# Three cross-attentions in eight-head units with 32-row score matmuls, each step's transposes issued first

## The chip, the cores and the metric

The kernel runs on one core of one Trainium2 chip. The metric is the device time of one execution in microseconds (us): the median of the runs shown, smaller is better. A kernel here is one program in which five engines run their own instruction streams at the same time: TensorE (PE, matmuls; PEld is its weight load), VectorE (DVE), ScalarE (ACT), GpSimd (POOL) and SyncE (SP, which only issues transfers). They meet at semaphores.

## What is computed

A decoder of four layers over 16 sequences of 128 tokens, width 128. Each layer is self-attention (or a recurrence), cross-attention and feed-forward, every one of them added to x behind a layer norm. The change touches the cross-attentions of layers 0, 1 and 2 (called L0x, L1x, L2x): 16 heads of 8 features each, keys and values from a context `ctx`.

```python
qh, kh, vh = heads(q @ Wq + bq), heads(ctx @ Wk + bk), heads(ctx @ Wv + bv)   # L0x: relu, no bias
scores = einsum('bhqd,bhkd->bhqk', qh, kh) / sqrt(8)
scores = where(mask, -1e9, scores)                                            # L1x only
out = einsum('bhqk,bhkd->bhqd', softmax(scores), vh)
x = x + out @ Wo + bo                                                         # L0x: x + out
```

## The kernel before

All of x stays in SBUF (`X`). The phases in `PHASES` run one after another; every phase goes over four groups (`GROUPS`) of four sequences, three in a hardware loop and the last written out.

**A unit.** In L0x, L1x and L2x a group is 16 units, one for each sequence i and each block g of four heads. The query weights are laid out so that head 4g+j stands in rows 32j to 32j+7 of its own 128-row block, so queries and keys take four projections each (`keys`, `queries`), and `KD` holds the keys as a block pattern on zeros: 12 copies of 32 rows on ACT (L1034) and 4 on DVE (L1346) for each group write it. For one unit PE does one float32 matmul with 128 contraction rows and 512 columns (`scores1`, L550; in L1x a bf16 matmul adds the mask ahead of it, L549), DVE takes the row maximum (`take_max`, L1268) and subtracts it (`shift`, L1280), ACT does the exponential (L999), PE transposes the four 128x128 blocks (`transpose_p`, L559), ACT copies them out of PSUM (L1008), and PE multiplies each by the head's values (`product_v`, L579; a column of ones in `VE` gives the sum). A float32 matmul shows as two records, a transpose as one.

**The order on each engine** is written by hand. PE, in step u: scores of unit u+3, transposes of u+1, product of u. The scores rotate over three PSUM banks, so PE's next scores never wait for the exponential of the unit before. ACT: exponential of u+1, then the copy of u. DVE: maximum of u+1, then the subtraction of u, and `normalise` for each sequence. At the end of a group come the next group's projections and the copies into `KD`; the next group's first scores wait for them.

**Between phases.** POOL clears `KD` ahead of L0f and ahead of L1x (L490). The mask of L1x is loaded when L1a is done, and the context of L1x is queued on SP behind it. POOL converts the mask for each group (L513). Rows that are masked in full are mended on DVE in L1x (L1276, L1289, L1291) with one more matmul (L582).

## Time and profile before

| what | us |
|---|---|
| median of 2 runs (lowest, highest) | 2348.39 (2346.02, 2350.75) |
| the profiled execution | 2347.53 |
| its span in the trace | 2345.5 |
| PE busy | 1660.7 (71%) |
| DVE busy | 1427.9 (61%) |
| ACT busy | 879.8 (38%) |
| POOL busy | 91.5 (4%) |
| L0x, from the last x of L0a to its own last x | 196.8 |
| L1x, likewise | 236.9 |
| L2x, likewise | 207.0 |

The time of the profiled execution is its span and 2.0 us around it. A busy share is a mean over phases with different limits: the recurrence of layer 3 hardly uses PE, the attentions hardly leave it idle. The granted clock (PEclk) is TensorE's clock as a share of 2.4 GHz; 0.5 is the lower level, 1.2 GHz. In a timeline row the idle time ahead of an instruction stands in brackets with what ended it.

### The profile page before, as it was taken

How to read it: one execution, taken by the hardware profiler on the slowest of the kernel's cores; microseconds unless marked ns; L12 is line 12 of the kernel's file. 1: busy time of each engine (PE TensorE's matmuls, PEld its weight loads, DVE VectorE, ACT ScalarE, POOL GpSimd, SP SyncE). 2: the span in 40 equal slices, each digit the busy share in tenths (PEclk: the TensorE clock that was granted, in tenths of full speed). 3: DMA queues.
4: the chain of work that ended last, by engine and by line, in shares of the span. 5: the costliest groups of instructions: out<-in, count | busy, mean ns of one | idle time of the engine just before them, and what ended most of it. 6: DMA issues, size and time to landing. Idle time of an engine off the chain costs nothing.

```text
span 2345.5 us, 29947 instructions
## 1 busy us (share of the span) xinstructions
PE 1660.7 (71%) x9244; PEld 1220.6 (52%) x9244; DVE 1427.9 (61%) x4030; ACT 879.8 (38%) x1409; POOL 91.5 (4%) x82
## 2 busy tenths in 40 slices
PE   5988989997368888869995369899988880000366
PEld 4876876664237557646663247656666440000244
DVE  4544445667865655647776864556657536999445
ACT  4455354563333443434443432255544331010022
POOL 1000000001000000010000100000000000000001
PEclk9999999998679999989996675999989995555568
DMA  2000003000000000000000000000000012000100
GB/s 97 1 0 0 0 1 128 5 4 1 0 0 1 0 0 0 0 14 5 4 5 1 0 0 0 0 5 9 0 1 0 15 29 73 1 1 1 45 9 18
DMA packets 19262, 27.92 MB, mean 12 GB/s; under 512 B 3184, under 2 KB 14320, under 8 KB 18288
## 3 DMA queue, kind: packets, MB, share of 16 engines
q1 hardware_dynamic: 19184, 27.02, 3.4%
q8 instruction: 31, 0.51, 0.1%
q14 instruction: 47, 0.39, 0.1%
HBM read 21.51 MB, written 5.51 MB: 12 GB/s over the span
## 4 chain that ended last, share of the span: by engine, by line
issue 59%; PE 22%; DVE 13%; DVEq 2%; ACT 1%; POOL 1%; DMA 1%; SPq 0%; POOLq 0%; ACTq 0%
PE PSA L550 3%; PE PSA L579 3%; PE PSA L883 2%; PE PSA L559 2%; PE PSA L802 2%; DVE W L1736 2%; DVE W L1725 2%; DVE BIG L1729 1%; PE PSA L819 1%; DVE BIG L1732 1%; PE PSA L622 1%; PE PSA L856 1%; PE PSA L846 1%; PE PSA L778 1%; DVE W L1710 1%
## 5 line engine op out<-in xcount | busy, mean ns | idle before, releaser
L1268 DVE TENSOR_REDUCE MX<-PSA 128x4 f32<-128x512 f32 x320 | 220.9, 690 | 273.2 <-PE PSA L550 129.6
L579 PEld LDWEIGHTS PSA<-VE,PR 128*128 128x128 f32 x2048 | 252.7, 193 | 25.1 <-issue 17.1
L579 PE MATMUL PSA<-VE,PR 128*128 128x9 f32 x2048 | 258.4, 254 | 0.1
L999 ACT ACTIVATE TMP<-TMP 128x512 f32<-128x512 f32 x160 | 100.8, 630 | 338.6 <-DVE TMP L1280 338.6
L550 PE MATMUL PSA<-BIG,QK 128*128 128x512 f32 x384 | 202.2, 615 | 11.1 <-DVE QK L1352 11.1
L910 PE MATMUL PSA<-W,TMP 128*128 128x128 f32 x32 | 8.3, 441 | 263.5 <-DVE TMP L1761 263.5
L1008 ACT ACTIVATE PR<-PSA 128x512 f32<-128x512 f32 x320 | 186.5, 583 | 7.2 <-PE PSA L559 6.6
L999 ACT ACTIVATE PQ<-PQ 128x512 f32<-128x512 f32 x160 | 100.7, 629 | 179.4 <-DVE PQ L1280 179.4
L910 PEld LDWEIGHTS PSA<-W,TMP 128*128 128x128 f32 x32 | 7.1, 327 | 264.6 <-DVE TMP L1761 264.6
L559 PE MATMUL PSA<-K,TMP 128*128 128x128 f32 x640 | 100.5, 279 | 33.0 <-ACT TMP L999 32.2
L559 PEld LDWEIGHTS PSA<-K,TMP 128*128 128x128 f32 x640 | 71.5, 140 | 100.5 <-ACT TMP L999 97.3
L474 POOL TENSOR_TENSOR RSTD<-VEPS,HALF 128x4 f32<-128x4 f32 x50 | 50.4, 1007 | 1576.4 <-DVE VEPS L1241 1576.4
L1280 DVE TENSOR_TENSOR TMP<-PSA,MX 128x512 f32<-128x512 f32 x160 | 109.3, 683 | 2.5
L1280 DVE TENSOR_TENSOR PQ<-PSA,MX 128x512 f32<-128x512 f32 x160 | 109.3, 683 | 2.4
L1034 ACT ACTIVATE BIG<-PSA,COLS 32x512 f32<-32x512 f32 x144 | 97.6, 678 | 32.3 <-PE PSA L622 28.9
L765 PE MATMUL PSA<-K,BIG 128*128 128x128 f32 x128 | 31.7, 414 | 107.8 <-DVE BIG L1473 107.8
L539 PE MATMUL PSA<-QK,BIG 128*128 128x128 f32 x512 | 103.2, 283 | 3.5 <-DVE BIG L1370 3.5
L994 ACT ACTIVATE XNT<-PSA 128x512 f32<-128x512 f32 x44 | 26.1, 593 | 212.0 <-PE PSA L528 212.0
L559 PEld LDWEIGHTS PSA<-K,PQ 128*128 128x128 f32 x640 | 73.8, 142 | 60.9 <-ACT PQ L999 56.2
L559 PE MATMUL PSA<-K,PQ 128*128 128x128 f32 x640 | 99.2, 278 | 4.2 <-ACT PQ L999 4.2
L541 PE MATMUL PSA<-I,BIG 128*128 128x128 f32 x512 | 99.0, 275 | 0.0
L680 PE MATMUL PSA<-W 128*128 128x256 f32 x256 | 66.5, 425 | 41.6 <-ACT W L401 39.5
(309 smaller groups left out, 3436.4 us busy)
## 6 DMA issues: line engine op xcount, KB each, us to landing
CTX<-in_ctx_t SPq DMA_DIRECT2D x16, 256.0 KB, 3.1
W<-in_w SPq DMA_DIRECT2D x1, 2048.0 KB, 7.3
ROWS<-in_rows SPq DMA_DIRECT2D x1, 1744.0 KB, 12.2
W<-in_w SPq DMA_DIRECT2D x2, 768.0 KB, 9.4
W<-in_w SPq DMA_DIRECT2D x1, 1412.0 KB, 14.3
W<-in_w SPq DMA_DIRECT2D x2, 640.0 KB, 10.0
W<-in_w SPq DMA_DIRECT2D x2, 512.0 KB, 12.5
scratch_q<-BIG SPq DMA_DIRECT2D x4, 256.0 KB, 2.4
```

The lines of the kernel that those rows point to most:

```text
L474: pool.tensor_tensor(RSTD[:, 0, :], VEPS[:, 0, :], HALF[:], ALU.pow).then_inc(ln_rstd.sem, 1)
L539: pe.matmul(bank[:, tok(j)], KD[:, u, j, :], KT[:, g, tok(i)], start=True, stop=False, skip_group_check=True)
L541: mm = pe.matmul(bank[:, tok(j)], POS[:, u, j, :], I2[:], start=False, stop=True, skip_group_check=True)
L550: mm = pe.matmul(bank, QT[:, g, tok(i)], KD[:, u].rearrange("p j t -> p (j t)"), start=p != "L1x", stop=True, skip_group_check=True)
L559: mm = pe.transpose(PS[4 + u % 2][:, tok(j)], PQ[u % 2][:, tok(j)], ident)
L579: mm = pe.matmul(dst, PR[:, u % 2, tok(j)], val, start=True, stop=True)
L680: mm = pe.matmul(PS[1 + c % 4][:, tok(n, 256)], pe_table[:, P - 1 - 4 * m:2 * P - 1 - 4 * m], QB[:, m].rearrange("p r h -> p (r h)"), star ...
L999: act.activation(PQ[u % 2], PQ[u % 2], ACT.Exp, scale=scale).then_inc(exp_ready.sem, 1)
L1008: act.activation(PR[:, u % 2, :], PS[4 + u % 2], ACT.Copy).then_inc(p_ready.sem, 1)
L1034: act.activation(KD.rearrange("p (i g) j t -> p i g j t", g=HG)[r, :, g, j, :], tile(PS[K_BANK[g]][r]), func, bias=col(f"{p}.bk", g)[r]).t ...
L1268: dve.tensor_reduce(MX[:, tok(u % 4, 4)], tile(PS[1 + u % 3]), AX_X, ALU.max).then_inc(max_taken.sem, 1)
L1280: dve.tensor_tensor(tile(PQ[u % 2]), tile(PS[1 + u % 3]), last(m, P), ALU.subtract).then_inc(shifted.sem, 1)
```

## The change

For L0x, L1x and L2x the units are replaced; the other phases keep their code.

- A unit has eight heads of one sequence: 8 units a group (`HALVES`), 32 a phase, all written out with no hardware loop. The weights are no longer padded: one projection each for keys and queries. POOL writes `KM` from the projected keys `KN`, four copies of 128x512 with all but one head in four zeroed (`masked_keys`), so that two float32 matmuls of 32 contraction rows and 512 columns, on neighbouring 32-row strips and into two banks, give the eight heads' scores. Four banks hold two units' scores.
- DVE's maximum and subtraction and ACT's exponential work on 128x1024. Transposes and PSUM copies stay at 512, two to a unit, through banks 4 and 5, one each.
- PE's step m is: transposes of unit m+1, scores of unit m+2, product of unit m. ACT's is: exponential of m+1, copies of m. Everything else (projections, next norm's transposes, outputs) has its place in a step, over bank 7, and groups follow one another without a break. Keys, values and queries have two buffers.
- The mask is loaded at the start and converted once, in L0a. Rows masked in full get queries of zero (`SOME`, computed in L0x), which takes the mending operations and the matmul L582 out of L1x. POOL's clearing ahead of L1x moves ahead of L1f.

The core of the diff:

```diff
+                    sp.dma_start(MASK1[:], mask1.rearrange("b o q k -> q (b o) k")).then_inc(masks_loaded, 16)
             for p in run:
-                if p == "L1x":
-
-                    if run[0] != p:
-                        sp.wait_ge(x_updated.sem, x_updated.before[p])
-                    sp.dma_start(MASK1, mask1.rearrange("b o q k -> q (b o) k")).then_inc(masks_loaded, 16)
...
+            def masked_keys(p, new):
+
+                pool.wait_ge(k_ready.sem, k_ready.at(p, new))
+                for r in range(4):
+                    ins = pool.tensor_scalar(KM[:, new % 2, :, r, :], tile(KN[:, new % 2, :]), col("lane", r), None, ALU.mult)
+                ins.then_inc(km_ready.sem, 1)
...
-                if p in ("L0f", "L1x") and p != run[0]:
+                if p in ("L0f", "L1f") and p != run[0]:
 
                     pool.wait_ge(x_updated.sem, x_updated.before[p])
                     pool.memset(BIG[:, 0:8192], 0.0).then_inc(kd_zero, 1)
...
+                if p == "L0a":
+                    pool.wait_ge(masks_loaded, 32)
+                    pool.tensor_copy(MKB[:], MASK1[:]).then_inc(mask_ready, 1)
+                if p in CROSS3:
+                    ln_root(p, 0)
+                    for new in range(GROUPS):
+                        masked_keys(p, new)
+                        if new:
+                            ln_root(p, new)
+                    continue
...
-                else:
-                    if p == "L1x":
-                        pe.matmul(tile(bank), NEGI[:], mid(MKB[:, i, :]), start=True, stop=False, skip_group_check=True)
-                    mm = pe.matmul(bank, QT[:, g, tok(i)], KD[:, u].rearrange("p j t -> p (j t)"), start=p != "L1x", stop=True,
-                                   skip_group_check=True)
...
+                def scores(m):
+                    it, e = m // HALVES, m % HALVES
+                    i, h = e // 2, e % 2
+                    if e == 0:
+                        pe.wait_ge(q_ready.sem, q_ready.at(p, it))
+                        pe.wait_ge(km_ready.sem, km_ready.at(p, it))
+                    if m >= 2:
+                        pe.wait_ge(shifted.sem, shifted.at(p, 0, m - 2))
+                    banks = [PS[2 * (m % 2) + n] for n in range(2)]
+                    if p == "L1x":
+                        for n in range(2):
+                            pe.matmul(tile(banks[n]), NEGI[:], mid(MKB[:, it * GB + i, :]), start=True, stop=False, skip_group_check=True)
+                    for n in range(2):
+                        r = strip_of(2 * h + n)
+                        mm = pe.matmul(banks[n], QN[r, it % 2, tok(i)], KM[r, it % 2, i].rearrange("p r t -> p (r t)"),
+                                       start=p != "L1x", stop=True, skip_group_check=True)
+                    mm.then_inc(s1_psum.sem, 1)
+
+                def transposes(m):
+                    pe.wait_ge(exp_ready.sem, exp_ready.at(p, 0, m))
+                    for c in range(2):
+                        if m:
+                            pe.wait_ge(p_ready.sem, p_ready.at(p, 0, 2 * (m - 1) + c))
+                        for j in range(4):
+                            mm = pe.transpose(PS[4 + c][:, tok(j)], PH[:, m % 2, tok(4 * c + j)], ident)
+                        mm.then_inc(t_psum.sem, 1)
+
+                def product(m):
+                    it, n, h = m // HALVES, m // 2, m % 2
+                    if m % HALVES == 0:
+                        pe.wait_ge(v_ready.sem, v_ready.at(p, it))
+                    if h == 0 and n:
+                        pe.wait_ge(on_ready.sem, on_ready.at(p, 0, n - 1))
+                    for c in range(2):
+                        pe.wait_ge(p_ready.sem, p_ready.at(p, 0, 2 * m + c))
+                        for j in range(4):
+                            head = 8 * h + 4 * c + j
+                            mm = pe.matmul(PS[6][:, 9 * head:9 * head + 9], PT[:, m % 2, c, tok(j)],
+                                           VE2[:, it % 2, n % GB, head, :], start=True, stop=True)
+                    mm.then_inc(pv_done.sem, 1)
...
+                project_keys(0, PS[4])
+                project_queries(0, PS[5])
+                project_values(0, PS[6])
+                scores(0)
+                scores(1)
+                transposes(0)
+                for m in range(GROUPS * HALVES):
+                    it, e = m // HALVES, m % HALVES
+                    if m + 1 < GROUPS * HALVES:
+                        transposes(m + 1)
+                    if m + 2 < GROUPS * HALVES:
+                        scores(m + 2)
+                    product(m)
+                    more = it + 1 < GROUPS
+                    if e == 0 and more:
+                        project_keys(it + 1, misc())
+                        freed = k_ready, k_ready.at(p, it + 1)
...
+                def exp(m):
+                    act.wait_ge(shifted.sem, shifted.at(p, 0, m))
+                    act.activation(PH[:, m % 2, :], PH[:, m % 2, :], ACT.Exp, scale=float(HD) ** -0.5).then_inc(exp_ready.sem, 1)
+
+                def copies(m):
+                    if m >= 2:
+                        act.wait_ge(pv_done.sem, pv_done.at(p, 0, m - 2))
+                    for c in range(2):
+                        act.wait_ge(t_psum.sem, t_psum.at(p, 0, 2 * m + c))
+                        act.activation(PT[:, m % 2, c, :], PS[4 + c], ACT.Copy).then_inc(p_ready.sem, 1)
...
+                keys(0, PS[4])
+                if p != "L1x":
+                    queries(0, PS[5])
+                exp(0)
+                for m in range(GROUPS * HALVES):
+                    if m + 1 < GROUPS * HALVES:
+                        exp(m + 1)
+                    copies(m)
+                    if m:
+                        after(m - 1)
...
+                def softmax_inputs(m):
+                    s = PSA[:, 2 * (m % 2):2 * (m % 2) + 2, :].rearrange("p n (r t) -> p (n r) t", r=4)
+                    high = MX[:, 8 * (m % 2):8 * (m % 2) + 8]
+                    dve.wait_ge(s1_psum.sem, s1_psum.at(p, 0, m))
+                    dve.tensor_reduce(high, s, AX_X, ALU.max).then_inc(max_taken.sem, 1)
+                    dve.wait_ge(max_taken.sem, max_taken.at(p, 0, m))
+                    if m >= 2:
+                        dve.wait_ge(t_psum.sem, t_psum.at(p, 0, 2 * (m - 2) + 1))
+                    dve.tensor_tensor(tile(PH[:, m % 2, :], 8), s, last(high, P), ALU.subtract).then_inc(shifted.sem, 1)
...
+                values(0, PS[6])
+                next_moments(p, 0)
+                for u in range(GROUPS * HALVES):
+                    it, e = u // HALVES, u % HALVES
+                    softmax_inputs(u)
+                    if u == 0:
+                        next_normed(p, 0)
+                    if e == 0 and it:
+                        values(it, PS[7])
+                    if u >= 3 and u % 2:
+                        normalise(u // 2 - 1)
...
+                    if e == 5 and it and p != "L0x":
+                        update(it - 1)
+                    if e == 5 and p == "L1x" and it + 1 < GROUPS:
+                        queries(it + 1, PS[7])
+                    if e == 5 and it + 1 < GROUPS:
+                        next_moments(p, it + 1)
+                    if e == 7 and it + 1 < GROUPS:
+                        next_normed(p, it + 1)
```

## Rows read from the trace of the kernel before

**Rows 1.** Stage windows, the three cross-attentions; columns as the first line names them

```profile
core 0: us, PE busy (x) PEld busy (x) DVE busy (x) ACT busy (x) POOL busy (x), PEclk, DMA share, GB/s
377.10:573.90 196.80, 183.54 (x1008) 123.02 (x1008) 127.13 (x252) 107.28 (x181) 4.03 (x4) 0.99 0.10 41
1027.30:1264.20 236.90, 210.24 (x1152) 143.34 (x1152) 158.64 (x373) 111.31 (x193) 13.34 (x9) 0.95 0.03 7
1529.55:1736.50 206.95, 191.82 (x1056) 129.97 (x1056) 131.10 (x269) 109.67 (x185) 4.03 (x4) 0.97 0.01 4
```

**Rows 2.** Timeline, group starts in L0x: start us, us, engine, line, operation

```profile
389.35 0.69 DVE L1268 TENSOR_REDUCE MX<-PSA 128x4 f32<-128x512 f32 x1 [1.29 <-PE PSA L550]
390.20 0.69 DVE L1268 TENSOR_REDUCE MX<-PSA 128x4 f32<-128x512 f32 x1 [0.17 <-PE PSA L550]
...
437.66 0.69 DVE L1268 TENSOR_REDUCE MX<-PSA 128x4 f32<-128x512 f32 x1 [1.29 <-PE PSA L550]
```

**Rows 3.** Timeline, one steady step of L0x on the four engines

```profile
411.29 1.10 PE L550 MATMUL PSA<-BIG,QK 128*128 128x512 f32 x2
...
412.23 0.60 PE L559 MATMUL PSA<-K,PQ 128*128 128x128 f32 x4
412.43 0.69 DVE L1268 TENSOR_REDUCE MX<-PSA 128x4 f32<-128x512 f32 x1 [1.04 <-PE PSA L550]
...
412.67 1.05 PE L579 MATMUL PSA<-VE,PR 128*128 128x9 f32 x8
413.04 0.68 DVE L1280 TENSOR_TENSOR TMP<-PSA,MX 128x512 f32<-128x512 f32 x1
...
413.58 1.10 PE L550 MATMUL PSA<-BIG,QK 128*128 128x512 f32 x2
...
413.76 0.63 ACT L999 ACTIVATE TMP<-TMP 128x512 f32<-128x512 f32 x1 [1.21 <-DVE TMP L1280]
...
414.29 0.58 ACT L1008 ACTIVATE PR<-PSA 128x512 f32<-128x512 f32 x1
414.44 0.45 PEld L559 LDWEIGHTS PSA<-K,TMP 128*128 128x128 f32 x4 [0.58 <-ACT TMP L999]
```

**Rows 4.** Groups by form, wide operations elsewhere; count | busy, mean ns | idle before

```profile
L1571 DVE TENSOR_TENSOR QK<-PSA,K 128x1024 f32<-128x1024 f32 x8 | 9.8, 1221 | 3.9 <-PE PSA L778 3.9
...
L1116 ACT COPY BIG<-QK 32x1024 f32<-32x1024 f32 x16 | 16.7, 1042 | 3.1 <-DVE QK L1575 2.8
```

**Rows 5.** Timeline of DVE, the end of L1x: two dependent operations

```profile
1258.07 0.25 DVE L1295 RECIPROCAL RD<-OS 128x16 f32<-128x16 f32 x1
1258.40 0.29 DVE L1297 TENSOR_TENSOR ON<-OS,RD 128x128 f32<-128x128 f32 x1
```

**Rows 6.** Timeline, the start of L1x and POOL's first job in L1f

```profile
1027.37 6.92 POOL L490 MEMSET BIG<- 128x8192 f32 x1 [3.61 <-DVE X L1263]
...
1032.56 5.75 PE L622 MATMUL PSA<-CTX,W 128*128 128x512 f32 x8 [11.88 <-DMA CTX<-in_ctx_t]
...
1034.24 0.61 POOL L513 CAST MKB<-BIG 128x512 bf16 x1
...
1274.40 1.01 POOL L479 TENSOR_TENSOR RSTD<-VEPS,HALF 128x4 f32<-128x4 f32 x1 [46.57 <-DVE VEPS L1549]
```

**Rows 7.** Timeline of PE, mask and score matmul of one L1x unit

```profile
1053.79 0.38 PE L549 MATMUL PSA<-MKB,NEGI 128*128 128x512 bf16 x1
1054.01 1.02 PE L550 MATMUL PSA<-BIG,QK 128*128 128x512 f32 x2
```

**Rows 8.** Timeline of PE, the last matmuls of L0x's attention

```profile
565.38 1.10 PE L550 MATMUL PSA<-BIG,QK 128*128 128x512 f32 x2
...
570.51 1.95 PE L579 MATMUL PSA<-VE,PR 128*128 128x9 f32 x16
```

**Rows 9.** Windows at the end of L0x; PEclk is the third column from the right

```profile
571.00:572.00 1.00, 1.00 (x12) 1.00 (x11) 0.00 (x0) 0.98 (x2) 0.00 (x0) 1.00 0.03 8
572.00:573.00 1.00, 0.46 (x5) 0.37 (x4) 0.43 (x2) 0.61 (x1) 0.00 (x0) 0.77 0.00 0
```

More of the change, by code:

```diff
@@ L42 @@
 NEG = -1e9
-SMALL = ("L0a", "L0x", "L1x", "L2x")
+SMALL = ("L0a",)
+CROSS3 = ("L0x", "L1x", "L2x")
+HALVES = 8
 CROSS = ("L0x", "L1x", "L2x", "L3x")
@@ L391, in kd_zeroed @@
         def kd_zeroed(p):
-            return sum(q in run[1:run.index(p) + 1] for q in ("L0f", "L1x"))
+            return sum(q in run[1:run.index(p) + 1] for q in ("L0f", "L1f"))
         def strip_of(j):
@@ L579, in product_v @@
                     mm = pe.matmul(dst, PR[:, u % 2, tok(j)], val, start=True, stop=True)
-                if p == "L1x" and g == 3:
-                    mm = pe.matmul(PS[6 + i % 2][:, 144:288], ONES[:], VE[:, i].rearrange("p h d -> p (h d)"),
-                                   start=True, stop=True)
                 mm.then_inc(pv_done.sem, 1)
@@ new lines, in keys, with small @@
+            def keys(p, new, g):
+                act.wait_ge(k_psum.sem, k_psum.at(p, new, g))
+                act.activation(KT[:, g, :], PS[K_BANK[g]], ACT.Identity, bias=col(f"{p}.bk", g)).then_inc(k_ready.sem, 1)
+            def small(p, it, more):
+                act.wait_ge(q_ready.sem, q_ready.at(p, it, HG - 1))
+                for j in range(2):
+                    for ins in spread_q(act.copy, j):
+                        pass
+                    ins.then_inc(qd_ready.sem, 1)
+                for c in range(0, 16, 2):
+                    act.wait_ge(pos_psum.sem, pos_psum.at(p, it, c))
+                    act.activation(POS.rearrange("p u j s -> p (u j) s")[:, :, 8 * c:8 * c + 8],
+                                   PS[1 + c % 4].rearrange("p (s u) -> p u s", u=64), ACT.Copy).then_inc(pos_even.sem, 1)
+                    if c < 8:
+                        r = strip_of(c // 2)
+                        act.copy(KD.rearrange("p (i g) j t -> p i g j t", g=HG)[r, :, :, c // 2, :],
+                                 QT[r].rearrange("p g (i t) -> p i g t", i=GB)).then_inc(kd_ready.sem, 1)
+                exponentials(p, it, float(HD) ** -0.5)
+                if more:
+                    keys(p, it + 1, 0)
+                    keys(p, it + 1, 1)
+                act.wait_ge(ot_psum.sem, ot_psum.at(p, it))
+                act.activation(OT[:], PS[5], ACT.Copy).then_inc(ot_ready.sem, 1)
+                if more:
+                    keys(p, it + 1, 2)
+                    keys(p, it + 1, 3)
@@ L1190, in _ @@
                         scan(it)
-                if p in ("L1a", "L1x") and kd_zeroed(p):
+                if p in ("L1a", "L2a") and kd_zeroed(p):
                     act.wait_ge(kd_zero, kd_zeroed(p))
-                if p == "L0x" or p in ("L0a", "L2a", "L2x"):
+                if p == "L0a":
                     act.wait_ge(setup_pool, 1)
@@ L1338, in values @@
[L1338 to L1348 removed]
+                dve.tensor_copy(VE[:, :, :, 0:HD], PS[V_BANK].rearrange("p (b h d) -> p b h d", b=GB, h=H)).then_inc(v_ready.sem, 1)
@@ L1373, in first_keys @@
-                def first_keys():
-                    keys(p, it + 1, 0)
-                    keys(p, it + 1, 1)
-                attend(p, it, normalise, fill=first_keys if more else None)
-                if p == "L0x":
-                    dve.drain()
-                    add_to_x(p, it, ON[:])
+                dve.drain()
+                for j in range(2, 4):
+                    for ins in spread_q(dve.tensor_copy, j):
+                        pass
+                    ins.then_inc(qd_ready.sem, 1)
@@ L1900, in lay_out @@
     parts = {}
-    for p, t in (("L0a", "L0_attn"), ("L0x", "L0_xattn"), ("L1x", "L1_xattn")):
-        parts[f"{p}.q"] = strips(a[f"{t}_Wq"].T)
-        parts[f"{p}.k"] = strips(a[f"{t}_Wk"].T)
-        parts[f"{p}.v"] = a[f"{t}_Wv"].T
+    parts["L0a.q"], parts["L0a.k"], parts["L0a.v"] = strips(a["L0_attn_Wq"].T), strips(a["L0_attn_Wk"].T), a["L0_attn_Wv"].T
+    for n in "qkv":
+        parts[f"L0x.{n}"], parts[f"L1x.{n}"], parts[f"L2x.{n}"] = a[f"L0_xattn_W{n}"].T, a[f"L1_xattn_W{n}"].T, a[f"L2_xattn_W{n}"]
     parts["L0a.o"] = a["L0_attn_Wp"].T
@@ L1938, in lay_out @@
         for n in "qk":
-            b = strips(a[f"{p[:2]}_xattn_b{n}"]) if p in ("L1x", "L2x") else np.zeros(H * STRIP, np.float32)
-            c[f"{p}.b{n}"] = b.reshape(HG, P).T
+            c[f"{p}.b{n}"] = np.zeros((P, HG), np.float32)
+    for p in CROSS3:
+        for n in "qk":
+            c[f"{p}.b{n}"] = (a[f"{p[:2]}_xattn_b{n}"] if p != "L0x" else np.zeros(P, np.float32))[:, None]
+    c["lane"] = (np.arange(P)[:, None] // HD % 4 == np.arange(4)[None, :]).astype(np.float32)
     for n in "qk":
```

364 lines of the change are left out of this document (208 added, 156 removed), and 6 rows, old and new, of the table W_PARTS.

## The prediction

> **What bounds the kernel now.** I read the stage windows first, since the change touches three phases only. L0x takes 196.8 us, L1x 236.9, L2x 206.95, together 640.7 of the span; PE is busy in 183.5, 210.2 and 191.8 of them at a granted clock of 0.99, 0.95 and 0.97 [rows 1]. So in these phases PE is the bound, unlike in the whole, where its share is 71%. Next comes the timeline of one step of L0x. PE's scores start at 411.29, its transposes at 412.23, its products at 412.67 and the next scores at 413.58: 0.94 + 0.44 + 0.91 = 2.29 us a step, back to back, for four heads [rows 3]. Over the same time DVE and ACT have about 1.2 us of work each. Last, the seam between groups: first maximum of one group at 389.35, of the next at 437.66 [rows 2]: 48.3 us for 16 steps of 2.29 (36.6), so 11.7 us a group go to projections and the writing of the key pattern.
>
> For the comparison I count in steps of eight heads: 32 a phase, 96 in all. Before, such a step costs 640.7 / 96 = 6.67 us, seams, starts and ends included.
>
> **The new step, and what is queued behind what.** The redesign removes most of the seam: keys and queries are one projection each where there were four, the 16 small copies a group are gone, buffers are double. What decides is PE's order. In step m it has the transposes of m+1, then the scores of m+2. The transposes wait for exponential m+1, that for subtraction m+1, that for maximum m+1, that for scores m+1. The scores of m+2 need none of this, their banks are free since subtraction m, but they stand behind the waiting transposes on PE's queue. DVE's next maximum waits for them. So one step is a single closed chain through three engines, with nothing in it overlapped. Before, scores of u+3 stood ahead of the transposes and three banks were in turn.
>
> There is a second wait in it. Banks 4 and 5 take the transposes of one unit. Those of m+1 must find them emptied by the copies of m, and ACT has these behind exponential m+1, though their input is a step old. So both copies lie in the chain.
>
> The terms, at the full clock:
>
> - Maximum over 128x1024: 1.22 us, as DVE's other 128x1024 pass over PSUM [rows 4]. The subtraction depends on it; two dependent DVE operations of 0.25 start 0.33 apart [rows 5], so 0.08 more: 1.30.
> - Subtraction 1.22, then ACT starts 0.04 after its end (413.04 + 0.68, 413.76) [rows 3, 4]: 1.26.
> - Exponential: ACT's next instruction starts 0.53 after a 512-wide one (413.76, 414.29) [rows 3]. 512 columns more cost 1.04 - 0.60 = 0.44 by a 1024-wide copy of 1.042 us [rows 4]: 0.97.
> - First copy: 0.58, less the 0.10 by which ACT's operations overlap: 0.48. Second: 0.60 with its landing, 0.03 to PE [rows 3]: 0.63.
> - The second four transposes: 0.44. The first four run while ACT copies.
> - Scores: from the start of one matmul to the maximum, 411.29 to 412.43, 1.14 [rows 3]. Two of full height are 0.85 apart (389.35, 390.20) [rows 2]. No row shows two matmuls on different 32-row strips. The upper bound is one after the other, 2.00; the lower is side by side, 1.14. A float32 matmul is two records, and only the second record of the first and the first of the second are neighbours on different strips, so I take half the pair's extra: 1.57.
>
> Sum: 1.30 + 1.26 + 0.97 + 0.48 + 0.63 + 0.44 + 1.57 = **6.65**, bounds 6.2 and 7.1. PE's own work in it is 0.88 + 1.28 + 1.82 = 4.0 us; it is no longer the bound and waits.
>
> The Trainium skill, "TensorE: Matmul & The Clock Gate", part 3 (packing small matmuls), says that matmuls whose operands lie on different 32-row strips run concurrently and start some 4 ns apart; no row here shows such a pair. Taken in full it makes the step 6.2, the lower bound.
>
> **The clock.** This is the term I am least sure of. At the end of L0x PE runs its last 512-column matmul at 565.38 for 1.10 us; then only transposes and products with 9 columns follow, until 572.5, PE being busy almost throughout [rows 8]. The granted clock is 1.00 in the window from 571, 0.77 in the next and 0.50 after it [rows 9]: before it fell to 1.2 GHz PE had run transposes and products for some 5.5 us and no wide matmul. In the new step the scores take 1.3 of 6.65 us and are the only wide matmuls; 5.4 us lie between them, with the same two kinds of work and 2.6 us idle. That is nearly the same stretch, in every step. At the lower level PE's durations double: the first transposes end 0.40 after the copies, the second take 0.44 more, the scores 0.86 to 1.7 (1.29 at my half): 6.65 + 2.13 = **8.8**, bounds 7.9 and 9.65. Scores, back to back for 2.6 us at the lower level, may lift the clock again, so I take half of the steps at either level: **7.7**.
>
> **The rest of a phase.** Start: 12.3 us in L0x from the phase's beginning to the first maximum (377.10 to 389.35) [rows 1, 2]. The new one drops the pattern, but adds moments, a root and four POOL products of 128x512, each at least 0.61 by POOL's conversion [rows 6], in line: 2.4 and more, so 13.5 in L0x and L2x. In L1x the first projection waited for the context until 1032.56, 5.3 us after the phase's begin, since SP had it behind the mask's transfer [rows 1, 6]; with both moved, 9.7. From first to second maximum 3.5 (the second unit's scores are there; the next norm stands between). Then 30 steps. Then the last unit: 2.56 on DVE, 6.2 from its exponential through copies and two products, 0.6 to normalise, and 0.8 for x in L0x; in L1x and L2x outputs, projection and x take 1264.20 - 1258.40 = 5.8 instead [rows 1, 5]. Fixed parts: 27.3, 28.3 and 32.1, in all 87.7.
>
> The mask in L1x: two bf16 matmuls more ahead of the scores, 0.22 each (1053.79, 1054.01) [rows 7], in the chain: 0.44 a step, at half the steps 0.88: 30 x 0.6 = 18.
>
> At no cost: `normalise`, `update` and the norms on DVE stand after the subtraction, where DVE waits 4.1 us for the next scores (the fullest step has some 4.4 of them, a few tenths a group at most). Projections and outputs on PE come after the product, ahead of 2.6 us of idle; at a longer step this cover grows. POOL's clearing, 6.92 us, now ahead of L1f, ends at 1271.1 before POOL's first job there at 1274.40 [rows 6]. POOL's conversion of the whole mask, four times 0.61 or somewhat more, lies in L0a ahead of nothing urgent; SP's earlier transfer of the mask is the last of the first batch. What leaves L1x (mending on DVE, the matmul L582) was work on engines that now wait, so it gains nothing.
>
> **The sum.** Three phases: 87.7 + 90 x 7.7 + 18 = 799 against 640.7: +158. From the profiled execution's 2347.5 (the median is 2348.4) this gives **2505 us**, 6.7% slower.
>
> **The rivals**
>
> - *The clock holds.* For it: in L0x a step with 0.9 us of products keeps it at 0.99. Against it: rows 8 and 9. Step 6.65: 87.7 + 598.5 + 13 = 699, +58, 2406; with serial scores (7.1) 2447. Chance 0.22.
> - *The clock stays down, scores in series.* Step 8.8 to 9.65, +260 to +335: 2605 to 2680. For it: 32 rows are a quarter of the array. Chance 0.12.
> - *Side by side at full clock.* Step 6.2: +18, 2366, within 2%. Chance 0.06.
> - *The order doesn't bind*, the other side of the result: scores of m+2 start while the transposes wait, as the double banks would allow. Then PE's 4.0 to 4.4 us set the step: 87.7 + 90 x 4.2 + 13 = 479, -162, 2186. It decides once the step falls under (640.7 - 101) / 90 = 6.0 us, where the kernel would be no slower. Against it: in each step of the trace PE's scores, transposes and products run in the written order, and the products wait where their turn is. Chance 0.05.
>
> The Trainium skill, "TensorE: Matmul & The Clock Gate", part 2, states that matmuls stay in program order and only weight loads are pulled ahead; the trace agrees (scores, transposes, products, scores, 2.29 us a step).
>
> **How the numbers follow.** My case, clock low in about half of the steps (2450 to 2600), has 0.55. Range: from the clock-holds value 2400 up to 2630, which leaves out the two fast rivals and the upper part of the serial one. Two per cent, some 47 us, is about what a measurement of this kernel can tell from no change. Faster by more than 2%: 0.05; within 2%: the side-by-side rival and the lower edge of the clock-holds case, 0.09; slower: 0.86.
>
> **What would show it.** In the new trace: DVE's maximum idle before it for about 4 us or more in every step, released by the scores; PE idle ahead of the transposes, released by ACT; exponential followed by two copies with no gap; maxima 6.2 to 9.6 us apart. The pair of scores shows whether its end lies 1.14, 1.6 or 2.0 after its start. The windows' clock at 0.7 to 0.85 in these phases, against 0.95 and more, is my clock term; at 0.95 the first rival holds. Wrong at the root I am if maxima come less than 6 us apart or DVE does not wait for the scores.

## The result

The changed kernel takes 2601.86 us (median of 2 runs, 2599.13 to 2604.60) against 2348.39: a ratio of 1.107, 95% interval 1.101 to 1.113. It is slower, as predicted, by 253.5 us where 157 were forecast. The time is inside the range and 97 us over the value named.

First the whole page of the kernel after: busy time by engine, and TensorE's granted clock in 40 slices.

```profile
span 2597.3 us, 28054 instructions
...
PE 1818.9 (70%) x9060; PEld 1372.4 (53%) x9072; DVE 1333.1 (51%) x3654; ACT 777.1 (30%) x1193; POOL 166.0 (6%) x128
...
PEclk9999985555679999956665568656657998555578
```

PE's share is what it was (71% before, 70% now), and it does 184 instructions fewer, yet its busy time rose from 1660.7 to 1818.9 us. Only the clock line shows why: the slices of the three cross-attentions, mostly at 9 before, now stand mostly at 5 and 6.

The stage windows of the three changed phases, against [rows 1] (columns: stretch, its length, busy time of each engine with its instructions, granted clock, DMA share, GB/s):

```profile
376.21:657.82 281.61, 240.69 (x960) 178.59 (x964) 107.29 (x168) 75.83 (x113) 28.87 (x20) 0.55 0.07 26
1113.80:1417.33 303.53, 256.00 (x1072) 180.48 (x1072) 107.65 (x176) 74.18 (x117) 28.85 (x20) 0.60 0.01 4
1691.87:1983.34 291.47, 242.70 (x1008) 180.69 (x1008) 104.73 (x173) 75.96 (x113) 28.85 (x20) 0.58 0.01 3
```

L0x went from 196.8 to 281.6 us, L1x from 236.9 to 303.5, L2x from 206.95 to 291.5: 876.6 together against 640.7, so 235.9 of the 251.8 us by which the span grew lie here. The granted clock was 0.99, 0.95 and 0.97; it is 0.55, 0.60 and 0.58. With only two levels, 0.5 and 1, a mean of 0.55 is 90% of the time at the lower one; for L1x and L2x it is 80% and 84%.

One step of L0x, answering to [rows 3] (timeline: start, duration, engine, line; in brackets the idle time before and what ended it):

```profile
436.79 1.23 DVE L1542 TENSOR_REDUCE MX<-PSA 128x8 f32<-128x1024 f32 x1 [2.15 <-PE PSA L747]
...
438.05 1.23 DVE L1546 TENSOR_TENSOR BIG<-PSA,MX 128x1024 f32<-128x1024 f32 x1
...
439.31 1.06 ACT L1194 ACTIVATE BIG<-BIG 128x1024 f32<-128x1024 f32 x1 [4.17 <-DVE BIG L1546]
440.27 1.06 ACT L1201 ACTIVATE QK<-PSA 128x512 f32<-128x512 f32 x2
...
440.99 1.94 PE L757 MATMUL PSA<-K,BIG 128*128 128x128 f32 x8 [2.37 <-ACT QK L1201]
...
442.86 2.08 PE L747 MATMUL PSA<-BIG 32*128 32x512 f32 x4
...
444.87 3.58 PE L770 MATMUL PSA<-VE,QK 128*128 128x9 f32 x16
444.99 1.23 DVE L1542 TENSOR_REDUCE MX<-PSA 128x8 f32<-128x1024 f32 x1 [5.71 <-PE PSA L747]
```

Read downwards it is the closed chain of the prediction. Each row starts where the one above it gives its result: maximum 1.26, subtraction 1.26, exponential 0.96, first copy 0.72 (PE waited 2.37 us and ACT's copy released it, the second wait that the prediction named), eight transposes 1.87, both score matmuls 2.13, next maximum. The sum is 8.20 us, and 8.2 is the distance of the maxima in most steps of the phase. DVE was idle 5.71 us before the last row, released by the scores. Over the run that is its largest wait on PE (columns: us in total, times, longest):

```profile
DVE MX L1542 <- PE PSA L747: 455.8, 93, 10.5
```

### The profile page after: what moved, and what is told of

Same layout as the page of the kernel before. It is cut to its first block, busy times and chain, and to the rows that moved or that the text cites. A ratio compares the mean times of both kernels' runs of the same rounds, so it can differ in the third digit from the quotient of the medians.

```text
span 2597.3 us, 28054 instructions
## 1 busy us (share of the span) xinstructions
PE 1818.9 (70%) x9060; PEld 1372.4 (53%) x9072; DVE 1333.1 (51%) x3654; ACT 777.1 (30%) x1193; POOL 166.0 (6%) x128
## 4 chain that ended last, share of the span: by engine, by line
PE 45%; issue 32%; DVE 14%; ACT 5%; POOL 2%; DVEq 2%; DMA 0%; SPq 0%; POOLq 0%; ACTq 0%
PE PSA L770 7%; PE PSA L757 6%; PE PSA L747 5%; PE PSA L563 2%; PE PSA L598 2%; PE PSA L565 2%; DVE MX L1542 2%; PE PSA L928 2%; DVE BIG L1546 2%; PE PSA L1009 2%; PE PSA L945 1%; PE PSA L683 1%; PE PSA L578 1%; DVE W L1949 1%; DVE W L1938 1%
## 5 line engine op out<-in xcount | busy, mean ns | idle before, releaser
L1542 DVE TENSOR_REDUCE MX<-PSA 128x8 f32<-128x1024 f32 x96 | 117.6, 1225 | 455.8 <-PE PSA L747 455.8
L770 PEld LDWEIGHTS PSA<-VE,QK 128*128 128x128 f32 x1536 | 279.8, 282 | 112.1 <-issue 112.1
L770 PE MATMUL PSA<-VE,QK 128*128 128x9 f32 x1536 | 288.0, 326 | 0.0
L1194 ACT ACTIVATE BIG<-BIG 128x1024 f32<-128x1024 f32 x96 | 101.4, 1056 | 599.9 <-DVE BIG L1546 599.9
L757 PE MATMUL PSA<-K,BIG 128*128 128x128 f32 x768 | 182.8, 419 | 90.5 <-ACT QK L1201 82.5
L757 PEld LDWEIGHTS PSA<-K,BIG 128*128 128x128 f32 x768 | 154.1, 224 | 124.1 <-ACT BIG L1194 103.9
L747 PE MATMUL PSA<-BIG 32*128 32x512 f32 x384 | 167.8, 986 | 19.5 <-POOL BIG L493 19.5
L1443 DVE TENSOR_REDUCE MX<-PSA 128x4 f32<-128x512 f32 x128 | 88.4, 691 | 143.3 <-PE PSA L565 93.9
L1546 DVE TENSOR_TENSOR BIG<-PSA,MX 128x1024 f32<-128x1024 f32 x96 | 117.6, 1225 | 3.3
L891 PE MATMUL PSA<-K,BIG 128*128 128x128 f32 x128 | 31.0, 407 | 109.9 <-DVE BIG L1686 109.9
L1201 ACT ACTIVATE QK<-PSA 128x512 f32<-128x512 f32 x192 | 102.6, 584 | 3.1 <-PE PSA L757 3.1
L891 PEld LDWEIGHTS PSA<-K,BIG 128*128 128x128 f32 x128 | 23.7, 216 | 115.1 <-DVE BIG L1686 115.1
```

Of the source, the lines that this page charges most:

```text
L747: mm = pe.matmul(banks[n], QN[r, it % 2, tok(i)], KM[r, it % 2, i].rearrange("p r t -> p (r t)"), start=p != "L1x", stop=True, skip_group_ ...
L757: mm = pe.transpose(PS[4 + c][:, tok(j)], PH[:, m % 2, tok(4 * c + j)], ident)
L770: mm = pe.matmul(PS[6][:, 9 * head:9 * head + 9], PT[:, m % 2, c, tok(j)], VE2[:, it % 2, n % GB, head, :], start=True, stop=True)
L1194: act.activation(PH[:, m % 2, :], PH[:, m % 2, :], ACT.Exp, scale=float(HD) ** -0.5).then_inc(exp_ready.sem, 1)
L1201: act.activation(PT[:, m % 2, c, :], PS[4 + c], ACT.Copy).then_inc(p_ready.sem, 1)
L1443: dve.tensor_reduce(MX[:, tok(u % 4, 4)], tile(PS[1 + u % 3]), AX_X, ALU.max).then_inc(max_taken.sem, 1)
```

## Experiments

Each run had the kernel before beside it on its chip. Since the chips differ by up to 9 us in that kernel (2346.4 to 2355.7), I give each run as its distance from the kernel before on the same chip. For the changed kernel that is +253.5. All are single runs but the last version's, which has four. On that chip seven runs of the kernel before lie within 6.2 us and the four of the last version within 21.2, so differences of less than some 20 us need the trace beside them.

**My theory.** Two causes: the order on PE's queue makes a step a closed chain, and the lower clock stretches PE's part of it. **Rivals:** only the order costs; only the clock costs; the clock is low because PE waits, so it would rise by itself once the order is mended.

### 1. Scores first

```diff
+                    if m + 2 < GROUPS * HALVES:
+                        scores(m + 2)
                     if m + 1 < GROUPS * HALVES:
                         transposes(m + 1)
-                    if m + 2 < GROUPS * HALVES:
-                        scores(m + 2)
                     product(m)
```

> The changed kernel with one swap in PE's step: scores of m+2 ahead of the transposes of m+1; nothing else. If the single chain through the transposes (T(m+1), scores, maximum, subtraction, exponential, T(m+2)) sets the step, the step falls from 8.2 us to what PE itself needs, 0.88 + 1.0 + 1.82 = 3.7 us and some waits, 3.9 to 4.4, the granted clock in the three phases is back at 0.95 or more, and the time is 2180 to 2230 us. If the order doesn't matter and only the low clock does, the step stays at 6 us or more and the time above 2390.

Measured: 2525.3 us, +169.6. So the order costs something, but mending it alone gives back 84 us, where the chain theory expected over 370. The timeline of L0x shows why; the last two rows are from L1x near its end:

```profile
500.90 3.42 PE L770 MATMUL PSA<-VE,QK 128*128 128x9 f32 x16
...
504.69 2.08 PE L747 MATMUL PSA<-BIG 32*128 32x512 f32 x4 [0.37 <-issue]
...
506.69 1.97 PE L757 MATMUL PSA<-K,BIG 128*128 128x128 f32 x8
...
1312.92 1.22 DVE L1542 TENSOR_REDUCE MX<-PSA 128x8 f32<-128x1024 f32 x1 [1.36 <-PE PSA L747]
...
1317.14 1.23 DVE L1542 TENSOR_REDUCE MX<-PSA 128x8 f32<-128x1024 f32 x1 [1.73 <-PE PSA L747]
```

The windows of the same kernel, two in L0x and L2x and one in L1x between them:

```profile
420.00:600.00 180.00, 178.90 (x683) 136.22 (x684) 76.67 (x122) 53.65 (x80) 15.49 (x11) 0.50 0.01 3
1136.00:1144.00 8.00, 7.96 (x59) 6.13 (x58) 5.44 (x6) 3.65 (x7) 1.71 (x2) 1.00 0.01 2
...
1656.00:1880.00 224.00, 219.84 (x844) 167.97 (x842) 86.20 (x138) 62.35 (x93) 21.34 (x15) 0.50 0.01 3
```

PE is now busy in 178.9 of 180 us: the chain is open, and PE is the bound. But the clock was 0.50 in all of it, and PE's work for a step is 7.1 us there (3.42 + 2.08 + 1.97 less the overlaps). In a few stretches of L1x, as in 1136 to 1144 and 1309 to 1317, it was 1.00, and in the second of these the maxima stand 4.22 us apart (1312.92, 1317.14) in a step without projections, the mask's matmuls included: the step that the prediction's last rival had for an order that does not bind (4.0 to 4.4 us). The rival that the clock recovers once PE no longer waits falls: PE has hardly any gap in these 180 us, and the clock stays down.

### 2. Copies before the exponential

ACT does the copies of unit m before the exponential of m+1, so both leave the chain except for the transposes' own wait.

```diff
-                    if m + 1 < GROUPS * HALVES:
-                        exp(m + 1)
                     copies(m)
+                    if m + 1 < GROUPS * HALVES:
+                        exp(m + 1)
```

> The changed kernel with one swap in ACT's step: the copies of unit m ahead of the exponential of m+1. The second wait of my chain (transposes of m+1 stand until ACT has copied unit m, and it copies after the exponential): if it is in the chain, the transposes start about 1.1 us after the exponential's start where they now start 1.68 after it, each step is 0.5 to 0.6 us shorter and the time 2545 to 2560 us. If not, it stays within 10 us of 2602.

Measured: 2582.7 us, +227.0, so 27 us better by the distances and 23 us over the upper end of what I had written. The timeline of L0x, in a step without projections:

```profile
503.99 1.06 ACT L1194 ACTIVATE BIG<-BIG 128x1024 f32<-128x1024 f32 x1 [3.27 <-DVE BIG L1546]
...
505.10 1.97 PE L757 MATMUL PSA<-K,BIG 128*128 128x128 f32 x8 [1.79 <-ACT BIG L1194]
```

Exponential to transposes is 1.11 us in place of 0.96 + 0.72, and such a step is 7.65 us, 0.55 less than 8.20. So the second wait is real, and it is worth half a microsecond in a plain step. But only about half of the steps of L0x and L2x are plain; most others took 8.2 to 9.1 us. In one of 9.13 us PE ran a projection when the exponential had started, from 512.44 on, and the transposes, which would have followed at 512.75, came at 514.28: the shorter wait no longer covers such work. The three phases took 858.8 us together against 876.6, 18 less and not the 50 that 90 steps of 0.55 would give.

### 3. Both score matmuls on one strip

```diff
-                        r = strip_of(2 * h + n)
+                        r = strip_of(2 * h)
```

The second matmul of a unit takes the heads of the first one's strip, so half of the heads get others' scores; the amount of work is the same.

> The changed kernel with both score matmuls of a unit on the same 32-row strip (so half the heads get another head's scores; shapes, banks and counts are the same). If the two strips run side by side in the changed kernel (four records in 1.2 us at the full clock, 2.1 at the lower), they now run one after the other: 0.86 or 1.7 us more a step, 75 to 155 us in all, 2680 to 2755. If the strips change nothing, the time stays at 2602.

Measured: 2758.0 us, +402.3. PE's timeline of L0x:

```profile
506.70 3.78 PE L747 MATMUL PSA<-BIG 32*128 32x512 f32 x4
```

At the same clock level the four records took 3.78 us, where on neighbouring strips they took 2.08. The step rose by 1.69 us, from 8.20 to 9.89. So in the changed kernel the pair does run side by side. (The Trainium skill, "TensorE: Matmul & The Clock Gate", part 3 on packing small matmuls, says so; the traces agree: 1.13 us for the pair at the full clock and 2.08 at the lower, about the time of one matmul.)

### 4. Added matmuls in the changed order

After each product, 6 bf16 matmuls of 128 rows and 512 columns go into the score bank that is free. Their result is overwritten.

```diff
                     product(m)
+                    if m + 1 < GROUPS * HALVES:
+                        pe.wait_ge(shifted.sem, shifted.at(p, 0, m + 1))
+                        for _ in range(6):
+                            pe.matmul(tile(PS[2 * ((m + 1) % 2)]), ONESB[:], mid(ONESB[:]), start=True, stop=True)
```

> The changed kernel with work added: six bf16 matmuls of 128 rows and 512 columns after each product, into a score bank that is free then, read by nobody; 1.3 us of PE at the full clock, 2.6 at the lower. If the low clock is what lengthens the step from about 6.2 to 8.2, the clock goes up to 0.9 or more, the step falls to 6.1 to 6.6 and the time to 2420 to 2470 us, although PE has more to do. If the clock is a bystander or stays down, the added work exceeds the 0.7 us that PE is idle in a step, each step grows by up to 1.9 us and the time is 2650 to 2780.

Measured: 2467.4 us, +111.7. Work that nobody needs makes the kernel 142 us faster, by the two distances. In 440 to 600 us the granted clock was 0.84. With 9 of them:

> The changed kernel's own order (transposes first), with 9 added wide matmuls after each product in place of 6 (2467.4 us at a granted clock of 0.8 to 0.9). It measures my prediction's chain at the full clock: with a clock of 0.95 or more throughout, DVE's maxima should stand 6.2 to 6.4 us apart where no projection comes between (6.2: 1.26 + 1.26 + 0.96 + 0.48 + 0.6 + 0.44 + 1.17), PE's 3.9 + 9 x 0.22 = 5.9 lies just under that, and the run takes 2400 to 2440. If the order is what costs and not the clock, it stays over the kernel before (2356) by 50 us or more. If only the clock cost, it comes to 2360 or less.

Measured: 2450.7 us, +104.3, and 11 us over the upper end of what I had written. Its windows in the three phases:

```profile
420.00:600.00 180.00, 175.47 (x1027) 109.72 (x1028) 85.09 (x133) 60.34 (x92) 16.71 (x12) 0.93 0.01 4
1110.00:1310.00 200.00, 195.84 (x1186) 123.52 (x1184) 90.49 (x144) 61.24 (x93) 21.66 (x15) 0.98 0.02 5
1630.00:1820.00 190.00, 184.60 (x1126) 118.51 (x1124) 88.53 (x141) 63.80 (x97) 21.67 (x15) 0.96 0.01 4
```

and the timeline of a step in L0x:

```profile
456.66 1.23 DVE L1546 TENSOR_REDUCE MX<-PSA 128x8 f32<-128x1024 f32 x1 [3.29 <-PE PSA L747]
457.92 1.23 DVE L1550 TENSOR_TENSOR BIG<-PSA,MX 128x1024 f32<-128x1024 f32 x1
...
459.18 1.06 ACT L1198 ACTIVATE BIG<-BIG 128x1024 f32<-128x1024 f32 x1 [4.34 <-DVE BIG L1550]
...
460.15 1.06 ACT L1205 ACTIVATE QK<-PSA 128x512 f32<-128x512 f32 x2
...
460.87 1.06 PE L757 MATMUL PSA<-K,BIG 128*128 128x128 f32 x8
...
461.87 1.13 PE L747 MATMUL PSA<-BIG 32*128 32x512 f32 x4
...
463.04 1.23 DVE L1546 TENSOR_REDUCE MX<-PSA 128x8 f32<-128x1024 f32 x1 [2.58 <-PE PSA L747]
```

This is the chain at the full clock: 1.26 + 1.26 + 0.97 + 0.72 + 1.00 + 1.17 = 6.38 us. With 6 added matmuls the plain step is 6.37 us, so it is not the added work that sets it. The kernel is still 104 us slower than before, 96 of them in the three phases (737.0 against 640.7), with a clock near the old one in these windows: "only the clock costs" (2360 or less) falls. The 104 us are not the price of the order alone. Over the whole phases, starts and ends included, the clock was 0.88, 0.92 and 0.91 against 0.99, 0.95 and 0.97, and each phase had one early step of 9.9 to 10.9 us.

### 5. Scores first and added matmuls

> Scores of unit m+2 stand before the transposes of m+1 on PE, and 3 idle-purpose matmuls (bf16, 128x512) follow each product. Theory A (two causes, the order and the clock, and they multiply): scores first alone ran at 0.50 of the clock in L0x (416 to 600 us) with steps of 7.1 to 9.0, but at 1.00 in 1136 to 1148 and 1334 to 1345, with steps of 4.2 to 5.2. If 3 added wide matmuls keep the clock up, a step is some 4.7 + 3 x 0.22 = 5.4 us and the run comes to 2310 to 2360, about the kernel before (2356). If they do not, PE is the bound at the low level with still more work: 2525 + 90 x 0.9 = about 2600. Rival B (the clock follows from PE's total load, which scores first raised from waiting to 100 per cent busy): low again, 2560 to 2620.

Measured: 2372.8 us, +26.4, 13 us over theory A's range. The same steps ran at either level, by three windows of L0x:

```profile
412.00:450.00 38.00, 37.64 (x136) 25.27 (x134) 12.47 (x22) 9.99 (x15) 7.09 (x5) 0.50 0.00 1
458.00:566.00 108.00, 107.71 (x691) 76.43 (x691) 69.86 (x103) 47.34 (x72) 14.46 (x10) 0.93 0.02 6
566.00:580.00 14.00, 14.00 (x58) 10.56 (x55) 5.45 (x6) 4.06 (x6) 0.00 (x0) 0.50 0.01 1
```

After two short ones of 3.4 and 4.2 us, the steps of L0x took 8.4 to 10.2 us for 56 us, then 4.4 to 5.3, and the last four, in the group that has no projections, 8.4 to 8.8. PE was busy throughout.

> Scores first, and 6 added wide matmuls a step. Theory A: clock at 0.95 or more in the three phases, step 4.7 + 6 x 0.22 = 6.0 us, PE-bound, run 2370 to 2410, slower than with 3 if 3 suffice, far faster than 2525. Rival B: clock low, PE at the low level with 2.6 us more a step: over 2650.

Measured: 2332.5 us, 13.9 under the kernel before and 38 to 78 under what I had written: I had added them to a step of 4.7 us read in L1x, where the mask's two matmuls are in it. In L0x the plain step with 6 is 5.08 us, with 3 it is 4.43: 0.22 for each added matmul and 3.78 for the rest.

With runs 1 and 4 this gives a table of two causes, as distance from the kernel before:

| | no added matmuls | 6 added |
|---|---|---|
| transposes first | +253.5 | +111.7 |
| scores first | +169.6 | -13.9 |

The order is worth 84 us at the low clock and 126 with the added work; the added work is worth 142 in the one order and 184 in the other. Each is worth some 42 us more once the other is mended, as far as four single runs can say. The 126 are not the order alone either: over the steps of L0x and L2x the clock was 0.82 and 0.84 with transposes first and 0.96 with scores first. In L1x it was nearly the same, 0.95 and 0.99, and there the phase took 251.0 and 216.4 us: 35 us for the order in one phase. At the low level PE's own 7.1 us stands just under the chain's 8.2 and hides most of the order's price.

### 6. What the added matmuls have that the scores lack

The scores are wide too (512 columns), and in run 3 they took 3.78 us of a step. So I made them serial and put them first:

> Scores first, and both score matmuls of a unit take the same 32-row strip, so they run one after the other (the output is not the reference's: the second takes the strip of the first); no filler. The pair takes 2.0 us in place of 1.17 at the full clock. If serial scores count for the clock as the kernel before's did (0.94 of 2.29 us a step at 0.99): clock up, step about 4.7 + 0.85 = 5.55, run 2330 to 2380. If 32-row matmuls do not hold it in whatever order: PE-bound at the low level, step 7.1 + 1.9 or more, run 2660 to 2740.

Measured: 2723.3 us, +376.9, half of the heads computed from the wrong strip. PE was busy for 179.3 of the 180 us from 420 to 600, scores taking 3.78 of an 8.82 us step, at a clock of 0.50. In the kernel before, scores take 0.94 of a 2.29 us step [rows 3], about the same share, at 0.99 [rows 1]. One difference is that there each matmul has 128 rows; another is that only 1.35 us of other work lie between the scores there, and some 5 us here. To change the height alone, I repeated the run with scores first and 6 added matmuls, and made these 32 rows high:

```diff
-                            pe.matmul(tile(PS[2 * ((m + 1) % 2)]), ONESB[:], mid(ONESB[:]), start=True, stop=True)
+                            pe.matmul(tile(PS[2 * ((m + 1) % 2)]), ONESB[strip_of(2 * ((m + 1) % 2)), :], mid(ONESB[strip_of(2 * ((m + 1) % 2)), :]), start=True, stop=True)
```

> As the run with scores first and 6 added matmuls (2332.5 us, clock 0.95 and more in the steady steps), but each added matmul has only 32 rows: 32x128 weights and 32x512 columns of the same bf16 tile, on the strip that the bank's scores use. The instruction count, the columns and PE's busy time are the same, the rows are a quarter. If the clock goes with PE's busy time or with wide matmuls as such: the same run again, 2325 to 2345. If it goes with how much of the array works, as the serial scores on one strip suggest (2723.3 us at a clock of 0.694 although PE was busy without a gap): clock low in the steady steps, PE-bound, 9 to 11 us a step, 2700 to 2850.

Measured: 2814.5 us, +461.7. Windows of this run in L0x and L2x:

```profile
420.00:600.00 180.00, 180.00 (x616) 117.45 (x615) 56.22 (x86) 40.20 (x60) 14.45 (x10) 0.50 0.01 3
...
1900.00:2150.00 250.00, 250.00 (x858) 163.67 (x856) 73.51 (x116) 53.65 (x80) 15.48 (x11) 0.50 0.01 3
```

and of the run with 128 rows in L0x and L2x:

```profile
420.00:560.00 140.00, 139.56 (x925) 95.12 (x927) 85.80 (x132) 58.56 (x89) 15.51 (x11) 1.00 0.02 5
...
1560.00:1700.00 140.00, 138.46 (x922) 95.24 (x922) 80.70 (x133) 57.16 (x86) 15.51 (x11) 1.00 0.02 5
```

The same number of instructions in the same order, PE with hardly a gap in both, 0.50 in one and 1.00 in the other, 476 us apart by their distances from the kernel before. In this kernel neither PE's busy time nor 512-column matmuls as such tell the clock; the height of the matmuls was the only thing changed between these two runs. L1x points the same way without any change of mine, since its mask puts two matmuls of 128 rows and 512 columns into each step: with 3 added matmuls the clock over its steps was 0.98 where L0x and L2x had 0.75 and 0.74. With about the same share of the step held at 0.99 by the 128-row scores of the kernel before, this points to the 32-row scores as what took the clock away, more than to the wait that the order adds. The changed kernel with its scores padded to 128 rows, which would show it outright, was not run. (The Trainium skill, "TensorE: Matmul & The Clock Gate", part 1, says that the gate goes by how busy PE has been recently. This pair of runs does not follow it if busy is read as the profile's busy time.)

### 7. A version that beats both

Scores first; 5 added matmuls a step in L0x and L2x and 3 in L1x, where the mask gives two of 128 rows; and DVE makes the first group's masked keys, which POOL had taken 6.19 us for, behind its root.

```diff
-                    for new in range(GROUPS):
+                    for new in range(1, GROUPS):
                         masked_keys(p, new)
...
+                dve.wait_ge(k_ready.sem, k_ready.at(p, 0))
+                for r in range(4):
+                    ins = dve.tensor_scalar(KM[:, 0, :, r, :], tile(KN[:, 0, :]), col("lane", r), None, ALU.mult)
+                ins.then_inc(km_ready.sem, 1)
```

> Scores first, 5 added matmuls a step in L0x and L2x and 3 in L1x (where two 128-row mask matmuls stand in each step anyway, and where the clock held with 3), and the first group's masked keys are made by DVE at the phase start in place of POOL (1.55 us each there, behind a 1.0 us root; DVE's tensor_scalar of this shape took 0.47). By the two-cause theory: 2332.5, less 60 x 0.22 and 30 x 0.66 for the fillers, less 8 us at each start = about 2275 (2260 to 2290). If 5 do not hold the clock in L0x and L2x as 3 did not at their starts: 2330 to 2400.

> The same with 24 more added matmuls ahead of the first scores of each phase, in PE's wait for the keys. In the runs so far each phase of L0x and L2x began at 0.50 and one early step took 10 to 11 us before the clock rose. If work ahead of the start lifts it: one such step less in each phase, minus 4 to 6 us each against the run without them, 2255 to 2275. If those 24 just delay the first scores (24 x 0.43 = 10 us at the low level against some 6 us of wait): no gain or 5 us a phase slower, 2275 to 2295.

Measured: 2314.8 us, -38.0 (this run is called tuned_cold below), and with 24 more matmuls ahead of each phase's first scores 2325.1, -27.8. DVE took 1.67 us for the four masked keys, and the first maximum of L0x came 7.2 us after the last x of L0a in place of 16.8. But the run without the 24 came out 25 us over the upper end of what I had written. Beside the run with 6, the steps of L1x took 182.3 us where I expected 20 less than 179.7, since it began with four steps of 9.3 to 11.3 us; and L2a, which the change does not touch, took 164.6 us where it had taken 154.1, at a clock of 0.74 for 0.80. The 24 matmuls delayed the first scores (L0x's first maximum from 385.9 to 390.1) and the early low-clock step of 10.3 us remained; warming that way gains nothing here.

> As tuned_cold (2314.8 us beside 2352.8 for the kernel before), but with 6 added matmuls a step in L1x's first group and 3 in its later groups. In tuned_cold L1x began with four low-clock steps of 11.3, 10.1, 9.3 and 10.2 us before it rose; with 6 (and the mask's two) only the first was near that (6.5, 6.0, 5.5, 7.0). By the two-cause theory the four steps shrink to about one of 11 and three of 6: minus 12 us or so, 2300 (2290 to 2315), 1.9 to 2.3 per cent under the kernel before. If the start's level in L1x has another cause than the added work: 2310 to 2320.

Measured, with 6 in L1x's first group: 2309.8 us (median of 4), ratio to the kernel before 0.9815, 95% interval 0.978 to 0.985, so faster by 1.5 to 2.2%; whether by more than 2% stays open. L1x's early steps were 12.0, 6.0, 5.5 and 7.0 as expected; three steps of 9.1 to 9.4 came later in the phase, so the gain over the run before is too small to claim. Its windows in L0x and the later part of L1x:

```profile
385.00:560.00 175.00, 169.27 (x1099) 116.91 (x1099) 105.30 (x162) 74.36 (x111) 22.70 (x16) 0.96 0.08 30
...
1050.00:1205.00 155.00, 152.14 (x954) 104.09 (x953) 85.45 (x138) 56.87 (x86) 15.49 (x11) 0.93 0.02 6
```

The redesign does pay, then, by a little and with conditions: the scores stand ahead of the transposes, and something 128 rows high keeps the clock up. With these two alone (6 added matmuls) a single run was 13.9 us, 0.6%, under the kernel before, too little to claim; the clear gain came with the shorter starts (7 to 8 us to the first maximum in place of 15 to 17) and fewer added matmuls.

## Why the prediction was right, and where it was not

**The closed chain: right.** Maximum, subtraction, exponential, both copies, transposes and scores follow each other as foretold, and DVE waits for the scores. At the full clock the step is 6.38 us against 6.65, at the lower 8.20 against 8.8.

**The pair of scores: mis-sized.** I took 1.57 us, half-way between side by side and serial, on the argument that only neighbouring records could overlap. It measured 1.17 at the full clock (461.87 to 463.04), the lower bound. The traces give the whole matmuls side by side.

**Transposes: mis-sized the other way.** I let the first four run while ACT does its second copy and counted 0.44 for the second four. The copies and transposes took 0.72 + 1.00 = 1.72 us where I had 0.48 + 0.63 + 0.44 = 1.55.

**The clock: right in kind, wrong in its share.** Half of the steps at the lower level was a guess; the granted clock of the three phases says 80 to 90%. The guess rested on the scores lifting it again, because they are wide. The runs with 32-row added matmuls show the hidden premise that failed: 32-row matmuls did not lift it. [rows 8, 9] had shown the fall after transposes and products only, so they could not tell width from height. Nor could they tell either from idling: PE's last product there ends at 572.46 (570.51 + 1.95), and a mean of 0.77 in that window puts the fall at 572.54. The steps took 762 us where the prediction had 711: 51 of the 97 us. These 51 are what is left of errors in two directions. With all 90 steps at the lower level the sum rises by 99 us, with 8.20 in place of 8.8 for such a step it falls by 54, and the mask adds 8: 764, beside the 762 measured. That the low step was put too long hid half of the clock's error, and that is luck.

**The mask: right.** 0.43 us a step at the full clock (6.81 against 6.38 in the run with 9 added), 0.85 at the lower (9.05 against 8.20), by 0.44 and 0.88.

**Fixed parts: too small by 27 us** (114.3 against 87.7). POOL's rows at the start of L0x:

```profile
383.50 1.01 POOL L487 TENSOR_TENSOR RSTD<-VEPS,HALF 128x4 f32<-128x4 f32 x1 [42.63 <-DVE VEPS L1416]
384.58 6.19 POOL L493 TENSOR_SCALAR BIG<-BIG,COLS 128x512 f32<-128x512 f32 x4
```

Each masked-key product took 1.55 us; I had "at least 0.61" from a conversion of the same size and used the bound as the value, 11 us short over three phases. In L1x the first maximum came 17.7 us after the phase's begin where I had 9.7. The early context load did its part: PE's first projection started at 1113.90, 0.10 us after the last x of L1a, where it had waited 5.3 us before. But with that wait gone L1x begins as L0x does, for which I had 13.5. The 9.7, 3.8 us less, is my own slip. At the ends, the last two products run at the lower clock:

```profile
649.55 6.83 PE L770 MATMUL PSA<-VE,QK 128*128 128x9 f32 x32
```

6.83 us where the prediction had two times 1.82, full-clock products as in [rows 3]; 14.2 us from the last maximum to the end of L0x against 10.2, and 18.9 against 15.2 in the other two.

**What I had at no cost: nearly right.** The phases outside the change grew by 15.9 us in all, 6.9 of them in L2a and 3.4 in L1a. For about 2, in L1f, the cause is below. L2a goes with the clock: 162.2 us at 0.76 against 155.3 at 0.79, and over the runs above the same code took 149.2 us at 0.84 and 166.4 at 0.73. Why its level differs from run to run, and what the rest is, stays open.

**The rivals.** "Clock holds" (2406) was in effect run with 9 added matmuls: the clock at 0.93 to 0.98 in the middle of the phases and 2450.7 us; the plain step held (6.38), but each phase began with two steps at the lower level or on the way up (8.2 to 10.9 us), and the fixed parts came to 104 us, not 87.7. It is slower than before too, so the verdict did not hang on the clock. "The clock stays down, scores in series" had 2605 at its lower edge, 3 us from the result, by luck: the clock was down, but the pair took 2.13 us at that level, side by side. "The order doesn't bind" was run as well: it is right about the step where the clock is at 1.00, and its 2186 us never came, because it took that clock for the whole.

## What to carry to other kernels

Look at what stands behind a waiting instruction on an in-order queue before looking at any duration: one swap of two lines was worth 84 to 126 us here. A change that makes matmuls shorter in rows can pay for its saved time with the clock of everything around it, so read the granted clock of each stage, and do not take a busy PE as proof of a fast one. Two costs that share a resource hide each other: test their mending together, not only one by one.

## What the hardware showed that I had not expected

Two float32 matmuls of 32 rows on neighbouring strips took 1.13 us together at the full clock; on one strip 3.78 at the lower level against 2.08.

PE was busy for 180 of 180 us with six 32x512 matmuls in every step at a granted clock of 0.50, and for 139.6 of 140 us with six 128x512 ones at 1.00.

POOL's clearing ahead of L1f held up one operation of DVE (timeline):

```profile
1417.39 6.92 POOL L510 MEMSET BIG<- 128x8192 f32 x1 [96.70 <-DVE X L1438]
1417.43 1.90 DVE L1693 SCALAR_TENSOR_TENSOR BIG<-W 128x512 f32<-128x512 f32 x3
1419.40 1.75 DVE L1695 TENSOR_REDUCE WSC<-BIG 128x3 f32<-128x1536 f32 x1
...
1422.39 3.00 DVE L1702 TENSOR_SCALAR BIG<-W,WSC 128x512 f32<-128x512 f32 x3
```

The three tensor_scalars of L1702 took 3.00 us where the same three took 1.28 before; the first of them lasted 2.21 us in place of 0.48, until 1424.60, 0.28 us after the clearing's end, and the other two followed it. The operations of L1693 and L1695 took as long as before beside the same clearing. (The Trainium skill, "SBUF — State Buffer", section "SBUF: two separate sides", has an exclusive lock on a port pair that DVE in its fast modes shares with GpSimd; the trace agrees with that for this one operation, which was held for 1.7 us.)
